# A gated delta layer in a decoder kernel: two column tiles at once in the block solve, output products between its parts, and two elementwise products on GpSimd

## The chip, the cores and the metric

The kernel runs on one core of a Trainium2 chip. The metric is the device time of one execution in microseconds; lower is better. The whole decoder is one program; the change touches one of its twelve sublayers.

## The reference

The program is a four-layer decoder on 2048 tokens of width 256. The sublayer concerned is the attention of layer 1, a gated delta rule with 16 batches of 128 tokens, 16 value heads in 8 key groups, head size 128, all in float32:

```python
def step(S, xs):                      # per batch and value head, token by token
    qt, kt, vt, gt, bt = xs
    S = S * jnp.exp(gt)[..., None, None]
    kv = jnp.einsum('bhk,bhkv->bhv', kt, S)
    delta = (vt - kv) * bt[..., None]
    S = S + jnp.einsum('bhk,bhv->bhkv', kt, delta)
    o = jnp.einsum('bhk,bhkv->bhv', qt * scale, S)
    return (S, o)
...
xf = o.astype(jnp.float32) * jax.nn.silu(z.astype(jnp.float32))
var = jnp.mean(xf * xf, -1, keepdims=True)
xn = xf * jax.lax.rsqrt(var + NORM_EPS) * norm_weight
return xn.reshape(B, T, VALUE_DIM) @ w_out.T
```

Ahead of it stand the projection of q, k, v and z, a causal convolution of four taps with SiLU, and the normalisation of q and k.

## The kernel before

The recurrence is not run token by token. For each batch and head, the 128 tokens form a lower triangular system: a 128x128 matrix of key products, weighted by decays and by beta, is inverted in blocks and applied to the values. A *round* `i` handles one key group for half of the batches: 8 batches times 2 value heads, 16 *slots* of 128x128. There are 16 rounds. In code, `h` is a half of a round (8 slots), `q` a quarter (4 slots, one bank of PSUM).

One round goes as follows. TensorE transposes the values (`turn_values`, L1214), multiplies keys with keys and queries (`multiply_keys`, L1220). VectorE multiplies the products by the decays `e` to get `aT` and `att` (L1653). GpSimd masks `aT` into `al` (L1187). The diagonal 16x16 blocks of `aT` go through memory into `blk` (SyncE's DMAs) so that VectorE can invert all of them at once (`invert`, from L1672), and the results come back through memory as `x0` and `xT0`. Meanwhile TensorE projects the next round's q, k and v (`project`, L1200), turns the previous round's gated outputs (`turn_output`, L1231), projects z (L1208), and multiplies the first half of the outputs by `wo` (`project_out`, L1237). VectorE, behind the inversion, scans the next round's decays (`scan`, L1648) and runs the next round's convolution as steps of one tap (`convolve`, L1593), adds the outputs to `x` (`add`, L1731), and makes `p1` (L1767).

The inverse is then put together from the blocks on TensorE in 64x64 tiles: products `e1`, `xT1`, `wT`, `xT2` (all L1243), each with a copy on ScalarE or VectorE behind it. Between `e1` and `xT1` stand the second half of the output products and the sums of squares of the next round's q and k (`sum_squares`, L1226), which need ScalarE's `squares` (L1448), which needs `silu` of the convolved q and k.

The block solve (`solve`) applies the inverse to the values: `upper` (L1261) for the first 64 rows, `across` (L1265) for their part in the last 64 rows, and `lower` (L1269) for the last 64 rows; ScalarE copies the results to `uw` (L1529, L1532) and VectorE adds (L1778). Then come the outputs (L1388), VectorE's gating with z (`gate`, L1718), and their sums of squares, from which ScalarE makes `rs` (L1470, L1472). `scale_gated` (L1726) multiplies the gated values by `rs`, for `turn_output` in the next round; `weigh` (L1640) multiplies the next round's decays by `beta`, behind ScalarE's exponential (`decay_exp`, L1452), for the next round's `aT`.

The order of work on each engine is written out by hand; engines wait for each other by semaphores, named after what has been done. The layer's work on TensorE, in order:

```python
previous_out(1)                      # L1368
if i:
    next_sums()
pe.wait_ge(s["p1_made"], i + 1)
...
solve(i)                             # L1384
```

Of the kernel before, what the change touches and what calls it, by code (L numbers as in the profile page):

```python
# [996 lines left out]
def layer1_delta(nc, g):  # L997
    with Layer(nc, "l1a") as L:
# [58 lines left out]
        def quarter(n):  # L1057
            return ps[:, 4 + n, :].rearrange("p (k n) -> p k n", n=128)

        in_rounds = gt[1].rearrange("p b h -> p (b h)")  # L1060

# [103 lines left out]
        @block.gpsimd  # L1165
        def _(pool):
            P = nc.gpsimd

            def scale_out(k):
                pool.wait_ge(s["wo_loaded"], 16 * k + 16)  # L1170
                P.tensor_scalar(wo[:], wo[:], nw[:, 0:1], -1.0, ALU.mult, ALU.mult).then_inc(s["wo_scaled"], 1)

            P.memset(raw[:, :, :, 0:CONV - 1], 0.0).then_inc(s["const"], 1)
            P.memset(eps[:], 1e-6).then_inc(s["const"], 1)
            P.memset(y[:], 0.0).then_inc(s["const"], 1)
            pool.wait_ge(s["const"], 3)
            P.memset(y[:, 0:PITCH:BLK + 1], 1.0).then_inc(s["zeroed"], 1)
            P.memset(x0[:], 0.0).then_inc(s["zeroed"], 1)
            P.memset(xT0[:], 0.0).then_inc(s["zeroed"], 1)
            pool.wait_ge(s["rest_loaded"], 16 * 4)  # L1180
            scale_out(0)
            for i in range(ROUNDS):
                for h in range(2):
                    if i:
                        pool.wait_ge(s["r_made"], 4 * i)
                    pool.wait_ge(s["a_made"], 2 * i + h + 1)
                    P.tensor_tensor(heads(al, h), heads(aT, h), bc(outer[:], 1, HALF), ALU.mult).then_inc(s["al_made"], 1)  # L1187
                if i % 2 == 0 and i:
                    scale_out(i // 2)

        @block.tensor
        def _(pe):
# [40 lines left out]

            def project_out(h):
                for b in range(4):
                    for r in range(2):
                        mm = MM(unit(h)[:, b * 256:(b + 1) * 256], oT[:, HALF * h + 2 * b + r, :], wo[:, r, :], start=r == 0, stop=r == 1)  # L1237
                mm.then_inc(s["out"], 1)

# [19 lines left out]
            def upper(q, k):  # L1259
                slot = 4 * q + k  # L1260
                return MM(quarter(q)[0:64, k, :], xT2[0:64, slot, :], vt[0:64, slot, :], start=True, stop=True)  # L1261

# [4 lines left out]
            def lower(q, k):  # L1267
                slot = 4 * q + k
                return MM(quarter(q)[64:128, k, :], xT2[64:128, slot, :], vt[64:128, slot, :], start=True, stop=True)  # L1269

            def solve(i):

                pe.wait_ge(s["xT2_out"], 2 * i + 1)
                for q in range(2):
                    for k in range(4):
                        mm = upper(q, k)
                    mm.then_inc(s["u_made"], 1)
                pe.wait_ge(s["xT2_out"], 2 * i + 2)
                for q in range(2):
                    pe.wait_ge(s["u_out"], 4 * i + q + 1)  # L1280
                    for k in range(3):
                        across(q, k)
                        upper(q + 2, k)
                    across(q, 3).then_inc(s["r_made"], 1)
                    upper(q + 2, 3).then_inc(s["u_made"], 1)
                for q in range(2):
                    pe.wait_ge(s["u_out"], 4 * i + q + 3)
                    pe.wait_ge(s["vr_made"], 4 * i + q + 1)
                    for k in range(3):
                        lower(q, k)  # L1290
                        across(q + 2, k)
                    lower(q, 3).then_inc(s["w_made"], 1)
                    across(q + 2, 3).then_inc(s["r_made"], 1)
                for q in range(2, 4):
                    pe.wait_ge(s["vr_made"], 4 * i + q + 1)
                    for k in range(4):
                        mm = lower(q, k)
                    mm.then_inc(s["w_made"], 1)

            def round_(i):  # L1300
# [39 lines left out]

                def previous_out(h):
                    if not i:
                        return
                    if h == 0:
                        pe.wait_ge(s["wo_scaled"], (i - 1) // 2 + 1)
                    pe.wait_ge(s["oT_out"], 2 * i - 1 + h)
                    project_out(h)

# [17 lines left out]
                for h in range(2):  # L1366
                    slot_half(4, h, diagonal(al), within(x0)).then_inc(s["e1_made"], 1)
                previous_out(1)  # L1368
                if i:
# [12 lines left out]
                if i == 0:  # L1382
                    next_sums()
                solve(i)  # L1384
                for h in range(2):
# [41 lines left out]
        def _(act):  # L1427
# [54 lines left out]
            def round_(i):  # L1482
# [44 lines left out]
                for q in range(4):  # L1527
                    act.wait_ge(s["u_made"], 4 * i + q + 1)
                    A(lows(uw, q), quarter(q)[0:64], ACT.Copy).then_inc(s["u_out"], 1)  # L1529
                for q in range(4):  # L1530
                    act.wait_ge(s["w_made"], 4 * i + q + 1)
                    A(highs(uw, q), quarter(q)[64:128], ACT.Copy).then_inc(s["w_out"], 1)  # L1532
            act.wait_ge(s["ba"], 1)
# [40 lines left out]
        def _(v):  # L1574
# [60 lines left out]

            def weigh(i, h):
                k, b0 = i // 2, batch0(i) + 4 * h
                t = heads(e, h).rearrange("p (b r) n -> p b r n", r=2)
                v.wait_ge(s["decay_exp"], 2 * i + h + 1)
                V.tensor_tensor(t, t, bc(beta[:, b0:b0 + 4, 2 * k:2 * k + 2], 3, 128), ALU.mult).then_inc(s["e_made"], 1)  # L1640

            def scan(i, h):
# [80 lines left out]

            def scale_gated(i, h):
                v.wait_ge(s["g_rs"], i + 1)
                V.tensor_tensor(heads(go, h), heads(go, h), bc(rs[:, HALF * h:HALF * h + HALF], 2, 128), ALU.mult).then_inc(s["normed"], 1)  # L1726

            def add(i, h):
# [7 lines left out]
            def round_(i):  # L1736
# [14 lines left out]
                for h in range(2):  # L1751
                    take_products(i, h, att, 1).then_inc(s["att_made"], 1)
                if i:
                    for h in range(2):
                        scale_gated(i - 1, h)
                invert(i)
# [14 lines left out]
                for h in range(2):  # L1771
                    v.wait_ge(s["xT2_made"], 2 * i + h + 1)
                    V.tensor_tensor(heads(xT2, h), half_out(3, h), heads(xT1, h), ALU.add).then_inc(s["xT2_out"], 1)
                if i:
                    add(i - 1, 1)
                for q in range(4):
                    v.wait_ge(s["r_made"], 4 * i + q + 1)
                    V.tensor_tensor(highs(vt, q), quarter(q)[64:128], highs(vt, q), ALU.add).then_inc(s["vr_made"], 1)  # L1778
                if more:
                    for h in range(2):  # L1780
                        weigh(i + 1, h)

# [8 lines left out]
            for h in range(2):  # L1791
                scan(0, h)
            for h in range(2):
                weigh(0, h)
            for i in range(ROUNDS):
# [2571 lines left out]
```

## Time and profile before

| | |
|---|---|
| median of the runs shown (2412.61 to 2426.64) | 2424.78 us |
| span of the profiled execution, first to last instruction | 2424.5 us |
| TensorE matmul busy | 2112.7 us (87%) |
| VectorE busy | 1856.6 us (77%) |
| ScalarE busy | 1477.2 us (61%) |
| GpSimd busy | 216.2 us (9%) |
| one steady round of the delta layer | 54.79 us |

The profiled execution's own time is its span; nothing else around it is recorded. Busy shares are averages over twelve sublayers with different limits. In the profile, PE is the matmul side of TensorE and PEld its weight load, DVE is VectorE, ACT ScalarE, POOL GpSimd and SPq SyncE's queue of DMA issues. A float32 product appears as two matmul records, and merged rows give the number of records as x16. In timelines the bracket tells the engine's idle time ahead of the row and what ended it.

### The profile page before, as it was taken

The page shows a single profiled execution, that of the slowest core. Times are in us where ns is not written, and L with a number is a line of the kernel's source. Part 1 is how long each engine was busy: PE and PEld are TensorE (multiplying, and loading weights), DVE is VectorE, ACT ScalarE, POOL GpSimd, SP SyncE. Part 2 cuts the span into 40 slices and gives each one's busy share as a digit, 9 for nine tenths or more (in the row PEclk, how much of TensorE's full clock was granted, in tenths as well). Part 3 has the DMA queues.
Part 4 walks back from the last instruction along what each step waited for, and adds up shares of the span by engine and source line. Part 5 has one row for each costly group of instructions (what it writes and reads, how often), then busy time and mean ns, then how long its engine had stood idle before and what let it go on. Part 6 is the DMA issues. An engine that isn't in the chain of part 4 may idle for free. (4 is left out here: it accounts for less than half of the span.)

```text
span 2424.5 us, 42274 instructions
## 1 busy us (share of the span) xinstructions
PE 2112.7 (87%) x16920; PEld 1596.5 (66%) x16920; DVE 1856.6 (77%) x3341; ACT 1477.2 (61%) x2466; POOL 216.2 (9%) x163
## 2 busy tenths in 40 slices
PE   7997447999999999999986589899999996888855
PEld 4666325777777777878774345788888873555633
DVE  4776667888989898889867834478888776678697
ACT  3664255667777777776736631577777775455365
POOL 0000100000100010101100042000000000100313
PEclk8998768999999999999988799999999996999977
DMA  3000012222222221222116355311010000200001
GB/s 159 2 1 12 13 34 53 72 83 57 64 56 66 56 64 54 62 74 80 36 49 212 129 143 176 115 32 57 23 27 6 5 18 1 81 2 1 16 1 35
DMA packets 164785, 135.14 MB, mean 56 GB/s; under 512 B 118512, under 2 KB 145776, under 8 KB 157936
## 3 DMA queue, kind: packets, MB, share of 16 engines
q1 hardware_dynamic: 160752, 126.02, 16.6%
q0 software_dynamic: 3840, 6.43, 1.4%
q8 instruction: 135, 2.21, 0.4%
q14 instruction: 58, 0.48, 0.1%
HBM read 106.42 MB, written 25.98 MB: 55 GB/s over the span
## 5 line engine op out<-in xcount | busy, mean ns | idle before, releaser
L1593 DVE SCALAR_TENSOR_TENSOR ctx_chan<-l1a_raw,l1a_cw,ctx_chan 128x1024 f32<-128x1024 f32 x192 | 232.0, 1279 | 3.5 <-issue 3.5
L1200 PE MATMUL banks<-x_chan,l1a_wp 128*128 128x512 f32 x512 | 225.2, 598 | 4.8 <-ACT l1a_vt L1488 4.8
L1200 PEld LDWEIGHTS banks<-x_chan,l1a_wp 128*128 128x128 f32 x512 | 98.0, 192 | 122.6 <-issue 116.7
L3166 PE MATMUL banks<-x_chan,more_weights_ahead 128*128 128x128 f32 x1024 | 123.6, 275 | 1.2 <-ACT l2a_kT L2693 1.2
L3166 PEld LDWEIGHTS banks<-x_chan,more_weights_ahead 128*128 128x128 f32 x1024 | 121.6, 192 | 3.9 <-ACT l2a_kT L2693 2.0
L1187 POOL TENSOR_TENSOR l1a_al<-l1a_aT,l1a_outer 128x1024 f32<-128x1024 f32 x32 | 75.0, 2364 | 483.2 <-DVE l1a_aT L1653 483.2
L1237 PE MATMUL banks<-l1a_wo,l1a_oT 128*128 128x256 f32 x512 | 117.7, 383 | 0.0
L2706 ACT ACTIVATE l2a_masked<-l2a_masked,l2a_rowmax 128x128 f32<-128x128 f32 x256 | 99.0, 392 | 28.9 <-DVE l2a_rowmax L2919 28.9
L3202 PE MATMUL banks<-l2a_wo,l2a_oT 128*128 128x256 f32 x512 | 114.5, 382 | 0.0
L1208 PE MATMUL banks<-l1a_wz,x_chan 128*128 128x256 f32 x512 | 113.4, 380 | 0.0
L3202 PEld LDWEIGHTS banks<-l2a_wo,l2a_oT 128*128 128x128 f32 x512 | 96.2, 190 | 14.3 <-issue 1.0
L1237 PEld LDWEIGHTS banks<-l1a_wo,l1a_oT 128*128 128x128 f32 x512 | 96.5, 191 | 13.6
L1208 PEld LDWEIGHTS banks<-l1a_wz,x_chan 128*128 128x128 f32 x512 | 96.4, 191 | 12.9 <-issue 0.5
L1436 ACT ACTIVATE l1a_raw<-banks 128x1024 f32<-128x1024 f32 x64 | 65.5, 1024 | 48.8 <-PE banks L1200 48.8
L126 PE MATMUL banks<-ident,x_tok 128*128 128x128 f32 x224 | 43.2, 357 | 40.2 <-ACT x_tok L194 18.4
L3470 ACT ACTIVATE l3a_probsT<-banks 128x512 f32<-128x512 f32 x64 | 38.1, 596 | 59.5 <-PE banks L3636 59.5
L1466 ACT ACTIVATE l1a_oT<-l1a_go 128x1024 f32<-128x1024 f32 x32 | 33.9, 1058 | 64.6 <-DVE l1a_go L1718 64.6
L1778 DVE TENSOR_TENSOR l1a_vt<-banks,l1a_vt 64x512 f32<-64x512 f32 x64 | 44.4, 694 | 37.1 <-PE banks L1265 37.1
L1648 DVE TENSOR_TENSOR_SCAN l1a_e<-ctx_tok 128x1024 f32<-128x1024 f32 x32 | 71.4, 2275 | 1.4 <-DMA ctx_tok<-l1a_rows_mem 1.4
L1438 ACT ACTIVATE ctx_chan<-banks,l1a_cw 128x1024 f32<-128x1024 f32 x64 | 71.0, 1110 | 0.0
L126 PEld LDWEIGHTS banks<-ident,x_tok 128*128 128x128 f32 x224 | 34.3, 185 | 48.7 <-ACT x_tok L194 19.8
L1265 PE MATMUL banks<-l1a_uw,l1a_al 64*64 64x128 f32 x512 | 65.4, 280 | 0.3 <-ACT l1a_uw L1529 0.3
(648 smaller groups left out, 5644.1 us busy)
## 6 DMA issues: line engine op xcount, KB each, us to landing
l1a_sq<-l1a_norm_mem SPq DMA_DIRECT2D x16, 1024.0 KB, 4.7
ctx_tok<-l1a_rows_mem SPq DMA_DIRECT2D x16, 1024.0 KB, 8.1
l1f_wgu<-in_l1f_wgu_dram SPq DMA_DIRECT2D x4, 1408.0 KB, 11.4
moe_sums<-l1x_zero SPq DMA_DIRECT2D x2, 2176.0 KB, 18.3
ctx_chan<-in_ctxT_dram SPq DMA_DIRECT2D x2, 2048.0 KB, 13.8
l1a_wp<-in_l1a_wp_dram SPq DMA_DIRECT2D x8, 512.0 KB, 5.5
l1f_wgu<-moe_sums SPq DMA_DIRECT2D x8, 512.0 KB, 7.5
x_chan<-in_xT_dram SPq DMA_DIRECT2D x4, 512.0 KB, 5.2
```

The source lines that it names most:

```text
L126: mm = nc.tensor.transpose(g.ps[:, n % 2, t * 128:(t + 1) * 128], g.x[:, t0 + t, c * 128:(c + 1) * 128], g.ident[:])
L1187: P.tensor_tensor(heads(al, h), heads(aT, h), bc(outer[:], 1, HALF), ALU.mult).then_inc(s["al_made"], 1)
L1200: mm = MM(projected(i, u)[:, q * 512:(q + 1) * 512], wp[:, c, u * 128:(u + 1) * 128], g.xT[:, c, t0:t0 + 512], start=c == 0, stop=c == 1)
L1208: mm = MM(unit(2 + h)[:, b * 256:(b + 1) * 256], g.xT[:, c, t0:t0 + S], wz[:, c, :], start=c == 0, stop=c == 1)
L1237: mm = MM(unit(h)[:, b * 256:(b + 1) * 256], oT[:, HALF * h + 2 * b + r, :], wo[:, r, :], start=r == 0, stop=r == 1)
L1436: A(raw[:, u, :, CONV - 1:], now, ACT.Copy)
L1438: A(conv[:, u, :], projected(i, u), ACT.Copy, scale=cw[:, c, CONV - 1:]).then_inc(s["tap"], 1)
L1593: V.scalar_tensor_tensor(t, raw[:, u, :, j:j + S], cw[:, c, j:j + 1], t, ALU.mult, ALU.add).then_inc(s["conv_done" if step == 2 else "conv ...
L1648: V.tensor_tensor_scan(heads(e, h).rearrange("p k n -> p (k n)"), rows[:, h * 1024:(h + 1) * 1024], floor, 0.0, ALU.add, ALU.max).then_inc ...
L2706: ins = A(probs[:, k, :], masked[:, k, :], ACT.Exp, bias=rowmax[:, k:k + 1], scale=128 ** -0.5, accum_out=rsum[:, k:k + 1])
L3166: mm = mm_(ps[:, 4 + q % 2, k * 128:(k + 1) * 128], wq[:, c, SHARE * q + k, :], g.xT[:, c, tile(i)], start=c == 0, stop=c == 1)
L3202: mm = mm_(ps[:, 6, 0:D], oT[:, h, :], wo[:, h, :], start=h == 0, stop=h == HEADS - 1)
```

## The change

Four things are changed in the delta layer, and nothing elsewhere.

1. In the solve, `upper` of quarters 0 and 1 alternate, and `lower` of quarters 2 and 3. For that, quarter 1's upper result is written to PSUM partitions 64 to 127 and quarter 3's lower result to partitions 0 to 63, so that the two use different column tiles of TensorE. ScalarE's copies read them there.
2. The second half of the output products is cut in four batches: two stay ahead of the sums of squares, one is issued behind the first upper products, one ahead of the last lower products. Its semaphore is raised at the end of the last one, and VectorE's `add(i - 1, 1)` stands behind the solve's additions instead of ahead of them.
3. `weigh` and `scale_gated` are issued on GpSimd instead of VectorE, behind the two `al` products of the round and ahead of `scale_out`.
4. The last lower products wait for all four of VectorE's additions at once.

```diff
+        def upper_rows(q):
+            return quarter(q)[64:128] if q == 1 else quarter(q)[0:64]
+        def lower_rows(q):
+            return quarter(q)[0:64] if q == 3 else quarter(q)[64:128]
...
+            def weigh(i, h):
+                k, b0 = i // 2, batch0(i) + 4 * h
+                t = heads(e, h).rearrange("p (b r) n -> p b r n", r=2)
+                pool.wait_ge(s["decay_exp"], 2 * i + h + 1)
+                P.tensor_tensor(t, t, bc(beta[:, b0:b0 + 4, 2 * k:2 * k + 2], 3, 128), ALU.mult).then_inc(s["e_made"], 1)
+            def scale_gated(i, h):
+                pool.wait_ge(s["g_rs"], i + 1)
+                P.tensor_tensor(heads(go, h), heads(go, h), bc(rs[:, HALF * h:HALF * h + HALF], 2, 128), ALU.mult).then_inc(s["normed"], 1)
...
+            pool.wait_ge(s["gates_made"], 2)
+            for h in range(2):
+                weigh(0, h)
             for i in range(ROUNDS):
                 for h in range(2):
                     if i:
                         pool.wait_ge(s["r_made"], 4 * i)
                     pool.wait_ge(s["a_made"], 2 * i + h + 1)
                     P.tensor_tensor(heads(al, h), heads(aT, h), bc(outer[:], 1, HALF), ALU.mult).then_inc(s["al_made"], 1)
+                if i:
+                    for h in range(2):
+                        scale_gated(i - 1, h)
+                if i + 1 < ROUNDS:
+                    for h in range(2):
+                        weigh(i + 1, h)
                 if i % 2 == 0 and i:
                     scale_out(i // 2)
...
-                for q in range(2):
-                    for k in range(4):
-                        mm = upper(q, k)
-                    mm.then_inc(s["u_made"], 1)
+                for k in range(3):
+                    upper(0, k)
+                    upper(1, k)
+                upper(0, 3).then_inc(s["u_made"], 1)
+                upper(1, 3).then_inc(s["u_made"], 1)
+                between(2, 3)
                 pe.wait_ge(s["xT2_out"], 2 * i + 2)
...
-                for q in range(2, 4):
-                    pe.wait_ge(s["vr_made"], 4 * i + q + 1)
-                    for k in range(4):
-                        mm = lower(q, k)
-                    mm.then_inc(s["w_made"], 1)
+                between(3, 4)
+                pe.wait_ge(s["vr_made"], 4 * i + 4)
+                for k in range(3):
+                    lower(2, k)
+                    lower(3, k)
+                lower(2, 3).then_inc(s["w_made"], 1)
+                lower(3, 3).then_inc(s["w_made"], 1)
...
-                previous_out(1)
+                previous_out(1, 0, 2)
                 if i:
                     next_sums()
...
-                solve(i)
+                solve(i, lambda first, stop: previous_out(1, first, stop))
...
-                    A(lows(uw, q), quarter(q)[0:64], ACT.Copy).then_inc(s["u_out"], 1)
+                    A(lows(uw, q), upper_rows(q), ACT.Copy).then_inc(s["u_out"], 1)
...
-                    A(highs(uw, q), quarter(q)[64:128], ACT.Copy).then_inc(s["w_out"], 1)
+                    A(highs(uw, q), lower_rows(q), ACT.Copy).then_inc(s["w_out"], 1)
...
-                if i:
-                    for h in range(2):
-                        scale_gated(i - 1, h)
                 invert(i)
...
-                if i:
-                    add(i - 1, 1)
                 for q in range(4):
                     v.wait_ge(s["r_made"], 4 * i + q + 1)
                     V.tensor_tensor(highs(vt, q), quarter(q)[64:128], highs(vt, q), ALU.add).then_inc(s["vr_made"], 1)
-                if more:
-                    for h in range(2):
-                        weigh(i + 1, h)
+                if i:
+                    add(i - 1, 1)
```

## Rows read from the trace of the kernel before

**Rows 1.** One steady round as one window: busy time of each engine, granted clock

```profile
core 0: us, PE busy (x) PEld busy (x) DVE busy (x) ACT busy (x) POOL busy (x), PEclk, DMA share, GB/s
875.87:930.66 54.79, 54.79 (x538) 42.90 (x537) 48.88 (x57) 39.16 (x45) 5.11 (x3) 1.00 0.22 60
```

**Rows 2.** Timeline of that round: start us, duration us, engine, line

```profile
877.62 3.62 PE L1220 MATMUL banks<-ctx_chan 128*128 128x256 f32 x16
...
881.28 1.23 DVE L1653 TENSOR_TENSOR l1a_aT<-banks,l1a_e 128x1024 f32<-128x1024 f32 x1 [0.45 <-PE banks L1220]
...
886.41 0.21 ACT L1472 ACTIVATE l1a_rs<-l1a_rs 128x16 f32<-128x16 f32 x1
...
889.58 0.18 DVE L1672 COPY l1a_y<-l1a_blk 128x8 f32<-128x8 f32 x1 [0.29 <-DMA l1a_blk<-l1a_blk_mem]
...
889.86 0.17 DVE L1677 TENSOR_TENSOR l1a_part<-l1a_blk,l1a_y 128x8 f32<-128x8 f32 x1
...
894.81 1.91 PE L1231 MATMUL banks<-ident,l1a_go 128*128 128x128 f32 x16
...
900.71 9.63 DVE L1593 SCALAR_TENSOR_TENSOR ctx_chan<-l1a_raw,l1a_cw,ctx_chan 128x1024 f32<-128x1024 f32 x8
900.83 1.06 ACT L1452 ACTIVATE l1a_e<-l1a_e 128x1024 f32<-128x1024 f32 x1 [1.02 <-DVE l1a_e L1648]
...
909.02 3.72 PE L1237 MATMUL banks<-l1a_wo,l1a_oT 128*128 128x256 f32 x16
909.90 1.91 ACT L1448 ACTIVATE l1a_sq<-ctx_chan 128x2048 f32<-128x2048 f32 x1
...
911.39 1.22 DVE L1767 TENSOR_TENSOR l1a_p<-l1a_ec,l1a_fold 128x1024 f32<-128x1024 f32 x1
...
912.67 1.07 PE L1226 MATMUL banks<-l1a_sq,ones 128*32 128x512 f32 x8
...
913.67 2.08 PE L1243 MATMUL banks<-l1a_xT,l1a_p 64*64 64x64 f32 x64
...
925.95 2.36 DVE L1640 TENSOR_TENSOR l1a_e<-l1a_e,l1a_beta 128x1024 f32<-128x1024 f32 x2
```

**Rows 3.** Timeline of TensorE in the block solve one round later

```profile
974.22 1.96 PE L1261 MATMUL banks<-l1a_vt,l1a_p 64*64 64x128 f32 x16
...
976.32 0.27 PE L1265 MATMUL banks<-l1a_uw,l1a_al 64*64 64x128 f32 x1
...
976.43 0.27 PE L1265 MATMUL banks<-l1a_uw,l1a_al 64*64 64x128 f32 x1
...
981.78 3.84 PE L1388 MATMUL banks<-l1a_uw,l1a_att 128*128 128x128 f32 x32
```

**Rows 4.** Line L1187, GpSimd's product: ns min/median/max of 32

```profile
L1187 POOL TENSOR_TENSOR l1a_al<-l1a_aT,l1a_outer x32: 2342/2363/2382, 377.1 to 1212.8; 128x1024 f32<-128x1024 f32 x32
```

**Rows 5.** Timeline of layer 3's tail, VectorE and GpSimd

```profile
2284.51 5.85 DVE L4092 SCALAR_TENSOR_TENSOR l3e_o<-l3e_o,l3e_rstd,more_weights_ahead 128x256 f32<-128x256 f32 x4
...
2328.51 1.67 DVE L4092 SCALAR_TENSOR_TENSOR l3e_o<-l3e_o,l3e_rstd,more_weights_ahead 128x256 f32<-128x256 f32 x4
```

**Rows 6.** The same stretch on GpSimd's own timeline

```profile
2284.62 2.59 POOL L3794 TENSOR_TENSOR more_weights_ahead<-more_weights_ahead,l3e_gb 128x1024 f32<-128x1024 f32 x1 [1.81 <-DVE l3e_o L4086]
2287.29 2.40 POOL L3796 TENSOR_TENSOR more_weights_ahead<-more_weights_ahead,l3e_gb 128x1024 f32<-128x1024 f32 x1
```

**Rows 7.** Line L1171 on GpSimd, first and seventh of eight, and VectorE beside it

```profile
336.04 0.70 POOL L1171 TENSOR_SCALAR l1a_wo<-l1a_wo,l1a_nw 128x512 f32<-128x512 f32 x1 [4.26 <-DMA l1a_wo<-in_l1a_wo_dram]
...
1093.21 2.23 POOL L1171 TENSOR_SCALAR l1a_wo<-l1a_wo,l1a_nw 128x512 f32<-128x512 f32 x1 [43.16 <-DMA l1a_wo<-in_l1a_wo_dram]
...
1092.61 2.35 DVE L1633 SCALAR_TENSOR_TENSOR ctx_chan<-ctx_chan,l1a_sq 128x1024 f32<-128x1024 f32 x2
```

**Rows 8.** TensorE after a long wait in the last round: timeline, windows

```profile
1217.73 3.67 PE L1231 MATMUL banks<-ident,l1a_go 128*128 128x128 f32 x16 [6.96 <-DVE l1a_go L1726]
...
1218.00:1220.00 2.00, 2.00 (x11) 0.50 0.27 74
```

More of the change, by code:

```diff
@@ L1232, in turn_output, with project_out @@
                 mm.then_inc(s["o_turned"], 1)
-            def project_out(h):
-                for b in range(4):
+            def project_out(h, first=0, stop=4):
+                for b in range(first, stop):
                     for r in range(2):
                         mm = MM(unit(h)[:, b * 256:(b + 1) * 256], oT[:, HALF * h + 2 * b + r, :], wo[:, r, :], start=r == 0, stop=r == 1)
-                mm.then_inc(s["out"], 1)
+                if stop == 4:
+                    mm.then_inc(s["out"], 1)
             def tile64(bank, lhsT, rhs, k, row):
@@ L1260, in upper @@
                 slot = 4 * q + k
-                return MM(quarter(q)[0:64, k, :], xT2[0:64, slot, :], vt[0:64, slot, :], start=True, stop=True)
+                return MM(upper_rows(q)[:, k, :], xT2[0:64, slot, :], vt[0:64, slot, :], start=True, stop=True)
             def across(q, k):
@@ L1268, in lower, with solve @@
                 slot = 4 * q + k
-                return MM(quarter(q)[64:128, k, :], xT2[64:128, slot, :], vt[64:128, slot, :], start=True, stop=True)
-            def solve(i):
+                return MM(lower_rows(q)[:, k, :], xT2[64:128, slot, :], vt[64:128, slot, :], start=True, stop=True)
+            def solve(i, between):
                 pe.wait_ge(s["xT2_out"], 2 * i + 1)
-                for q in range(2):
-                    for k in range(4):
-                        mm = upper(q, k)
-                    mm.then_inc(s["u_made"], 1)
+                for k in range(3):
[4 more added lines that the diff above has]
+                between(2, 3)
                 pe.wait_ge(s["xT2_out"], 2 * i + 2)
@@ L1339, in round_, with previous_out @@
                     gate_project(i, h)
-                def previous_out(h):
+                def previous_out(h, first=0, stop=4):
                     if not i:
@@ L1346, in previous_out @@
                     pe.wait_ge(s["oT_out"], 2 * i - 1 + h)
-                    project_out(h)
+                    project_out(h, first, stop)
                 def next_sums():
@@ L1634, in normalise @@
                                        ALU.mult).then_inc(s["kq_normed"], 1)
[L1636 to L1640, printed above, removed]
             def scan(i, h):
@@ L1722, in sum_gated @@
                 V.tensor_reduce(ss[:, HALF * h:HALF * h + HALF], heads(oT, h), AX.X, ALU.add).then_inc(s["gsum"], 1)
-            def scale_gated(i, h):
-                v.wait_ge(s["g_rs"], i + 1)
-                V.tensor_tensor(heads(go, h), heads(go, h), bc(rs[:, HALF * h:HALF * h + HALF], 2, 128), ALU.mult).then_inc(s["normed"], 1)
             def add(i, h):
@@ L1792, in _ @@
                 scan(0, h)
-            for h in range(2):
-                weigh(0, h)
             for i in range(ROUNDS):
```

## The prediction

> **What bounds the kernel now.** I read the profile's busy shares first, then one steady round of the delta layer as a single window, then the timeline of that round. In the window TensorE is busy for 54.79 of 54.79 us at the full granted clock, VectorE for 48.88 [rows 1]. So TensorE's instruction stream is the bound, and 16 rounds of it are some 880 us of the 2424.5. But a full TensorE is no proof of slack elsewhere, so the timeline is read for the second-latest path into each TensorE wait. It runs through VectorE. The product of keys ends at 881.24 and VectorE makes the second half of aT from it by 882.51; the diagonal blocks go to memory and back, and the first instruction of the inversion starts at 889.58, having waited 0.29 us for that transfer, not for VectorE. From there VectorE never stops: inversion, two scans, eight convolution steps (900.71 to 910.34), an addition, and p1, which ends at 912.61. TensorE starts the product that needs p1 (xT1) at 913.67, only 1.06 us later. The sums of squares start at 912.67, and their input was ready at 911.81, only 0.86 us earlier [rows 2]. So behind a bound of TensorE stands a second one, of VectorE plus a transfer, about one microsecond away.
>
> **The change part by part.** First, the pairing. Upper products of quarters 0 and 1, and lower products of quarters 2 and 3, run alone today: 16 records in 1.96 us. Two products on different column tiles start every 0.11 us together [rows 3], so 16 records as 8 pairs cost 8 x 0.11 + 0.1 = 0.98. Two places: 2 x 0.98 = 1.96 us less TensorE work per round.
>
> Second, the output products of the second half. They take 912.67 - 909.02 = 3.65 us ahead of the sums; half of them, 1.83, moves into the solve, a batch in each of two places where TensorE would otherwise wait for ScalarE's u copies and VectorE's additions (some 0.8 us each). The solve from its first product to the first of the outputs is 7.56 us (974.22 to 981.78) [rows 3]; after, 7.56 - 1.96 + 1.83, and 0.2 for four more changes between small tiles and the full array (0.1 for the way in and out, from 3.72 against 3.62 us for 16 records of one shape) [rows 2]: 7.63. So the solve is 0.1 longer, and the saving stands ahead of the sums. Bounds: 0.2 shorter if the changes cost nothing, 0.4 longer if an exposed copy is added. The Trainium skill, TensorEngine Tiling (Array Packing), Key Properties, says that changing the tiling mode drains TensorE. That rule speaks against products between tile products; the 0.1 us of the rows is all that the trace shows of it.
>
> Now TensorE comes to the sums at 910.85 instead of 912.67, but the squares end at 911.81 still, since they hang on VectorE's convolution through ScalarE. It starts at 911.87: a gain of 0.8, not 1.83, less the 0.1: 0.7 us a round, if VectorE's path stays as it is.
>
> Third, scale_gated. Off VectorE this saves nothing: its 2.35 us lay in the wait for the blocks' transfer. On GpSimd a product of this shape takes 2.36 us [rows 4] against 1.22. GpSimd is through with al at 885.7, rs comes at 886.62 [rows 2], so the two end at 891.34. TensorE wants them at 894.81 [rows 2]: 3.5 us to spare. The stride of zero in the broadcast is not in rows 4; I take 2.36, with 1.2 (VectorE's) and 3.5 as ends.
>
> Fourth, weigh. VectorE loses 2.36 us at 925.95 [rows 2], and gets add(i-1, 1) behind the solve (1.22). What waits for it next, the product of keys, comes after 16 transposes on TensorE, so this gains nothing on the path. On GpSimd the two products become ready with the decays, at 901.9 and somewhat over a microsecond later than that if the scans are late: in the middle of VectorE's convolution [rows 2]. What queues behind them on GpSimd is scale_out, then al of the next round, all early enough.
>
> **What that does to VectorE.** In layer 3's tail four VectorE instructions with two SBUF inputs and a per-partition scalar take 1.67 us alone, and 5.85 where two GpSimd products of 2.36 us run [rows 5]; the GpSimd ones start 0.11 us after the first of these and take 2.59 and 2.40 [rows 6]. VectorE stood still for 4.18 us, 2.09 for each product, and GpSimd got in between back-to-back instructions. The convolution step has the same form: two SBUF inputs, a scalar from cw. The other way round: a GpSimd scaling takes 0.70 us alone and 2.23 when it arrives while VectorE runs two back-to-back instructions with two SBUF inputs and no scalar; these keep their 2.35 [rows 7]. There GpSimd waited for both. Products with banks as one input ran beside al without a loss (aT, 1.23) [rows 2], so nothing is charged for them. The Trainium skill, SBUF — State Buffer, Who interferes with whom, states the same division: a VectorE instruction with two SBUF inputs contends with a GpSimd one that reads SBUF, one with a single SBUF input doesn't; and by its next rule issue order decides who blocks, which would leave both outcomes below open.
>
> Charged to VectorE's path, per round:
> - Inversion. L1677, with two SBUF inputs, is due at 889.86 and is held until GpSimd's second scaling ends at 891.34, less 0.14 of overlap: +1.3.
> - Convolution. Two GpSimd products get in, 2 x 2.09: +4.2.
> - Squares end at 911.81 + 5.5 = 917.3, sums take 1.07, xT1 starts at 918.4; p1 ends at 912.61 + 5.5 = 918.1 and doesn't decide. Against 913.67: +4.7, and 0.1 for the solve: +4.8.
> - TensorE now waits 917.3 - 910.85 = 6.5 us. After a wait of 6.96 us in the last round the granted clock is 0.50 (1.2 GHz) and 16 transposes take 3.67 us [rows 8] instead of 1.91 [rows 2]: +1.8. Ends: 0, and twice that, 3.6, if it stays low into the solve of small tiles.
>
> Sum: 6.6 us a round, in the 14 rounds (1 to 14) that have all parts: +92.4. Round 0 has the slower weigh in front of its first product (+1.3) and blocked convolutions of which idle time hides about 3 of 4.2; the last round has only the held inversion, 1.3 less what the pairing gives. Together +3. 2424.5 + 95.4 = 2519.9, so 2520. The span of the profiled execution, 2424.5, is within 0.3 us of the median of the runs shown, 2424.78, so the sum needs no correction.
>
> **The rivals.**
> - *GpSimd is kept out of the convolution.* Speaking for it: rows 7; against: the convolution's form is that of rows 5, not of rows 7. Then the first weigh starts beside add(i-1, 0) at about 911.6 and ends at 914.0, p1 is held to 915.0, and xT1 starts at 915.05: +1.4, with the solve +1.5 a round, 14 x 1.5 + 3 = +24: 2448. TensorE's wait is then 3 us, and if the clock falls too, +1.8 a round: 2474.
> - *Only the inversion is held,* because weigh falls in harmless gaps: sums at 913.15, +0.6 with the solve +0.7: 14 x 0.7 + 3 = +13: 2437.
> - *No holding at all: faster.* If the convolution and the small products run at their old speed (steps of 1.28 us) beside GpSimd, the 0.7 us a round stay: 14 x 0.7 = 10, less 1 for round 0: 2416. It decides as soon as the holdings add up to less than 0.7 us a round. At its far end the squares are early as well and all of the 1.96 less the 0.1 counts, 14 x 1.86 = 26: 2398. Rows 5 speak against it.
> - *The pairing doesn't pair.* Both tiles read the same rows of vt's partitions, as the across and upper pair does now, so rows 3 speak against it. It would cost 1.96 us in the solve, 14 x 1.96 = 27 on top of the forecast: 2547.
>
> **How the numbers follow.** GpSimd gets into both places: 0.60, from 2424.5 + 3 + 14 x 4.8 = 2495 to 2424.5 + 3 + 14 x 8.4 = 2545. GpSimd kept out of the convolution: 0.22, half of it below 2449. Inversion only: 0.06. No holding: 0.10, of which 0.04 at its far end. No pairing: 0.02. A measurement of this kernel can tell about 1%, 24 us, from no change. Faster by more: 0.04. Within: 0.06 + 0.06 + 0.11 = 0.23. Slower: 0.73. The range from 2435 to 2545 leaves out no holding below and a tail of about 0.07 above.
>
> **What the profile after would show.** Pairing right: 8 pairs of L1261 in about 1 us. Holding right: VectorE's L1677 of over a microsecond instead of 0.17, or a start that late; two of eight convolution steps of about 3.3 us instead of 1.28; TensorE waiting 5 to 7 us at L1226 for the squares, and a granted clock of 0.5 behind it; rounds of 60 to 62 us. The prediction is wrong if the convolution's durations are unchanged and GpSimd's weigh is long instead (the first rival, p1 late), or if neither is (the third).

## The result, and the profile after

The changed kernel takes 2503.27 us (median of 4, 2502.31 to 2505.78) against 2423.9 us before (median of 4): ratio 1.0345, interval 1.0323 to 1.0367 (the two medians by themselves give 1.0327, inside it). It is some 3.4% slower. Of all executions in this document one, of `weigh_on_vector`, ran in a slow state (3193.06 us at a granted clock of 0.639); the ratios leave it out, and the median of that kernel without it is 2426.80 instead of the 2427.24 given below. The profiled execution has a span of 2504.0 us against 2424.5, so 79.5 us are to be found in the traces. In the delta layer, from the first `al` product of round 1 to that of round 15, the time went from 770.31 to 849.31 us: 79.0 in 14 rounds, 5.6 a round. The rest of the program hardly moved.

The page's first part, engines' busy time over the span:

```profile
span 2504.0 us, 42224 instructions
...
PE 2114.7 (84%) x16869; PEld 1582.5 (63%) x16920; DVE 1845.7 (74%) x3279; ACT 1477.8 (59%) x2466; POOL 353.5 (14%) x225
```

GpSimd is up from 216.2 to 353.5 us and TensorE's busy time is unchanged within 0.1% (2112.7 before). VectorE's is only 10.9 us lower (1856.6 before), although 62 products of 1.2 us went, some 75 us. TensorE and VectorE were given no more work, and the kernel is slower, so the profile has to be read for waits and for instructions that take longer than they should.

One round of 59.81 us as a window, which answers to [rows 1] (columns as there, from one round's first transpose of values to the next's): TensorE, busy for all of 54.79 us before, now idles for 4.9. The mean of the 14 rounds is 60.7 us, against 55.0 before.

```profile
919.58:979.39 59.81, 54.95 (x539) 41.53 (x538) 48.38 (x53) 39.28 (x45) 14.20 (x7) 0.97 0.20 56
```

VectorE's own timeline of this round, which answers to the VectorE rows of [rows 2]:

```profile
933.26 0.93 DVE L1698 COPY l1a_y<-l1a_blk 128x8 f32<-128x8 f32 x1 [2.54 <-DMA l1a_blk<-l1a_blk_mem]
934.10 0.16 DVE L1700 COPY l1a_y<-l1a_blk 128x8 f32<-128x8 f32 x1
...
934.30 0.17 DVE L1703 TENSOR_TENSOR l1a_part<-l1a_blk,l1a_y 128x8 f32<-128x8 f32 x1
...
945.18 12.88 DVE L1625 SCALAR_TENSOR_TENSOR ctx_chan<-l1a_raw,l1a_cw,ctx_chan 128x1024 f32<-128x1024 f32 x8
957.99 1.21 DVE L1753 TENSOR_TENSOR x_tok<-banks,x_tok 128x1024 f32<-128x1024 f32 x1
959.12 1.20 DVE L1786 TENSOR_TENSOR l1a_p<-l1a_ec,l1a_fold 128x1024 f32<-128x1024 f32 x1
```

And GpSimd's two pairs of new products:

```profile
930.40 3.75 POOL L1196 TENSOR_TENSOR l1a_go<-l1a_go,l1a_rs 128x1024 f32<-128x1024 f32 x2 [1.04 <-ACT l1a_rs L1504]
944.25 5.56 POOL L1192 TENSOR_TENSOR l1a_e<-l1a_e,l1a_beta 128x1024 f32<-128x1024 f32 x2 [10.09 <-ACT l1a_e L1484]
```

Read them side by side. The inversion's first copy starts at 933.26, but takes 0.93 us instead of 0.18 [rows 2]: it ends at 934.19, and the first GpSimd pair ends at 934.15. The eight convolution steps take 12.88 us instead of 9.63: +3.25. GpSimd's second pair runs from 944.25 to 949.81, beside the end of the second scan and the first two of them. These two steps alone, from the same timeline in a shorter window:

```profile
945.18 5.71 DVE L1625 SCALAR_TENSOR_TENSOR ctx_chan<-l1a_raw,l1a_cw,ctx_chan 128x1024 f32<-128x1024 f32 x2
```

They take 5.71 us, 2.87 and 2.92 us each where the other steps take 1.27. The second scan and GpSimd's two products one by one:

```profile
943.00 2.27 DVE L1674 TENSOR_TENSOR_SCAN l1a_e<-ctx_tok 128x1024 f32<-128x1024 f32 x1
...
944.25 2.71 POOL L1192 TENSOR_TENSOR l1a_e<-l1a_e,l1a_beta 128x1024 f32<-128x1024 f32 x1 [10.09 <-ACT l1a_e L1484]
...
946.92 2.88 POOL L1192 TENSOR_TENSOR l1a_e<-l1a_e,l1a_beta 128x1024 f32<-128x1024 f32 x1
```

The two engines take turns. The scan keeps its 2.27 us although a product starts inside it; the product ends 1.69 us behind the scan, and the first step stands still meanwhile. The second product ends 1.77 us behind the first step, and holds the second step. So a product waits for the VectorE instruction that is running, and the next VectorE instruction waits for the product. In each of the 14 rounds two of the twelve steps take about 2.9 us, 28 in all; the line's minimum, median and maximum in ns:

```profile
L1625 DVE SCALAR_TENSOR_TENSOR ctx_chan<-l1a_raw,l1a_cw,ctx_chan x168: 1267/1272/2922, 459.0 to 1266.8; 128x1024 f32<-128x1024 f32 x168
```

What follows on ScalarE and TensorE (the squares, then the rest of the outputs, the sums, xT1, wT, and the solve from L1289 to L1420):

```profile
957.62 1.91 ACT L1480 ACTIVATE l1a_sq<-ctx_chan 128x2048 f32<-128x2048 f32 x1
```

```profile
952.73 1.99 PE L1264 MATMUL banks<-l1a_wo,l1a_oT 128*128 128x256 f32 x8
959.58 1.94 PE L1253 MATMUL banks<-l1a_sq,ones 128*32 128x512 f32 x8 [4.86 <-ACT l1a_sq L1480]
961.45 2.57 PE L1271 MATMUL banks<-l1a_xT,l1a_p 64*64 64x64 f32 x64
963.88 2.08 PE L1271 MATMUL banks<-l1a_xT,l1a_ec 64*64 64x64 f32 x64
...
967.69 1.09 PE L1289 MATMUL banks<-l1a_vt,l1a_p 64*64 64x128 f32 x16
968.71 1.13 PE L1264 MATMUL banks<-l1a_wo,l1a_oT 128*128 128x256 f32 x4
...
974.69 1.09 PE L1297 MATMUL banks<-l1a_vt,l1a_p 64*64 64x128 f32 x16
975.71 3.84 PE L1420 MATMUL banks<-l1a_uw,l1a_att 128*128 128x128 f32 x32
```

To compare with [rows 2], lay the two rounds together at the end of the second aT product: 926.21 here, 882.51 before, a shift of 43.70. The squares end at 959.53 - 43.70 = 915.83, before at 911.81: +4.0, which is the 0.73 of the copy and the 3.25 of the convolution. The sums start 3.2 later than before, since they had 0.86 to spare, and TensorE waits 4.86 us for them, where before it hardly waited. The wait in all rounds, total, times, longest:

```profile
PE banks L1253 <- ACT l1a_sq L1480: 68.8, 14, 5.6
```

Behind the wait, the granted clock (third column from the right) in windows of 2 us:

```profile
958.00:960.00 2.00, 0.42 (x4) 0.79 0.00 0
960.00:962.00 2.00, 2.00 (x18) 0.50 0.03 8
962.00:964.00 2.00, 2.00 (x64) 0.86 0.00 0
```

The sums take 1.94 us instead of 1.07, and xT1 starts 1.87 behind them instead of 1.00; its own step to the next line is 2.43 instead of 1.94. That is 1.4 us for the clock. The solve takes 975.71 - 967.69 = 8.02 us instead of 7.56: +0.5. The sum for this round is 3.2 + 1.4 + 0.5 = 5.1. In other rounds the low clock lasts longer, up to all of xT1 (3.68 us busy) and some of what follows. From the start of the sums to the start of the solve the 14 rounds take 8.10 to 9.51 us, 8.9 in the mean, against 6.75 in nearly all rounds before, so over the layer the low clock costs 2.2 us a round and not 1.4. With it the sum is 5.9 above the 54.79 of a steady round; the 14 rounds before took 55.0 in the mean, which leaves the 5.6.

### The profile page after: what moved, and what is told of

Same layout as the page of the kernel before. It is cut to its first block and busy times, and to the rows that moved or that the text cites. A ratio compares the mean times of both kernels' runs of the same rounds, so it can differ in the third digit from the quotient of the medians.

```text
span 2504.0 us, 42224 instructions
## 1 busy us (share of the span) xinstructions
PE 2114.7 (84%) x16869; PEld 1582.5 (63%) x16920; DVE 1845.7 (74%) x3279; ACT 1477.8 (59%) x2466; POOL 353.5 (14%) x225
## 3 DMA queue, kind: packets, MB, share of 16 engines
q8 instruction: 135, 2.21, 0.4%
## 5 line engine op out<-in xcount | busy, mean ns | idle before, releaser
L1625 DVE SCALAR_TENSOR_TENSOR ctx_chan<-l1a_raw,l1a_cw,ctx_chan 128x1024 f32<-128x1024 f32 x192 | 280.7, 1526 | 3.5 <-issue 3.4
L1264 PE MATMUL banks<-l1a_wo,l1a_oT 128*128 128x256 f32 x512 | 126.3, 391 | 0.0
L1192 POOL TENSOR_TENSOR l1a_e<-l1a_e,l1a_beta 128x1024 f32<-128x1024 f32 x32 | 87.6, 2757 | 194.0 <-ACT l1a_e L1484 194.0
L1253 PE MATMUL banks<-l1a_sq,ones 128*32 128x512 f32 x128 | 30.9, 1060 | 79.0 <-ACT l1a_sq L1480 79.0
L1474 ACT ACTIVATE ctx_chan<-ctx_chan 128x1024 f32<-128x1024 f32 x32 | 33.6, 1056 | 70.5 <-DVE ctx_chan L1625 68.6
L1679 DVE TENSOR_TENSOR l1a_aT<-banks,l1a_e 128x1024 f32<-128x1024 f32 x32 | 39.2, 1225 | 43.3 <-PE banks L1247 39.0
```

The source lines that it names most:

```text
L1192: P.tensor_tensor(t, t, bc(beta[:, b0:b0 + 4, 2 * k:2 * k + 2], 3, 128), ALU.mult).then_inc(s["e_made"], 1)
L1625: V.scalar_tensor_tensor(t, raw[:, u, :, j:j + S], cw[:, c, j:j + 1], t, ALU.mult, ALU.add).then_inc(s["conv_done" if step == 2 else "conv ...
```

## The experiments

Two theories stood against that of the held instructions. *Lateness*: GpSimd is slow, and somebody waits for its results. *Solve*: the new order of TensorE's work is longer. In all experiments "on VectorE" puts one half of `weigh` behind the xT2 additions and one behind the solve's additions. Each was timed beside runs of the kernel before on the same chip, which had a median of 2420.2 to 2420.8 us for all ten.

**weigh_on_vector.** `weigh` back on VectorE, `scale_gated` left on GpSimd.

```diff
-                if i + 1 < ROUNDS:
-                    for h in range(2):
-                        weigh(i + 1, h)              # GpSimd
+                if more:
+                    weigh(i + 1, 0)                  # VectorE, ahead of the solve's additions
                 for q in range(4):
                     v.wait_ge(s["r_made"], 4 * i + q + 1)
                     ...
+                if more:
+                    weigh(i + 1, 1)
```

> The changed kernel with weigh back on VectorE (one half behind the xT2 additions, one behind the solve's additions), scale_gated still on GpSimd. Holding theory (GpSimd's reads hold VectorE's instructions with two SBUF inputs): the two convolution steps of 2.92 us go back to 1.27, TensorE's wait for the squares and the low clock behind it go, only the held start of the inversion (0.8 us) stays: 2418 to 2432. Rival, the solve is what got longer (pairing and output products between): stays at 2495 to 2505. Rival, GpSimd is merely late (its products' results are awaited): falls too, so this run does not tell it from holding.

Measured: 2427.24 us, ratio 1.0026 (1.0011 to 1.0042). The solve theory falls: 76 of the 79 us are gone with the solve left as changed. All convolution steps of the 14 rounds are back at their old length (count, busy time, mean ns):

```profile
L1613 DVE SCALAR_TENSOR_TENSOR ctx_chan<-l1a_raw,l1a_cw,ctx_chan 128x1024 f32<-128x1024 f32 x168 | 203.0, 1279 | 0.0
```

**scale_on_vector.** The other way round: `scale_gated` back on VectorE behind the `att` products, `weigh` on GpSimd.

> The changed kernel with scale_gated back on VectorE, weigh still on GpSimd amid the convolution. Holding theory: the inversion's first copy is 0.18 us again, and starts at the transfer: 0.8 us a round less, 14 x 0.8 = 11 below the changed kernel: 2488 to 2496, with the two convolution steps still at 2.9 us. Solve theory: no change, 2500 to 2506.

Measured: 2488.96 us, ratio 1.0288 (1.0255 to 1.0321). The first copy of the inversion is short again in every round (minimum, median, maximum in ns), and the eight convolution steps still take 12.88 us:

```profile
L1691 DVE COPY l1a_y<-l1a_blk x15: 174/175/178, 446.9 to 1282.8; 128x8 f32<-128x8 f32 x15
```

```profile
935.35 12.88 DVE L1618 SCALAR_TENSOR_TENSOR ctx_chan<-l1a_raw,l1a_cw,ctx_chan 128x1024 f32<-128x1024 f32 x8
```

So `scale_gated` on GpSimd costs 14 us beside `weigh`, and 11 us without it (2427.24 against 2416.06 below). Given the intervals of the ratios these two don't differ; 14 rounds of 0.73 us would make 10.

**weigh_late.** All of the change, with one more wait:

```diff
                 if i + 1 < ROUNDS:
+                    pool.wait_ge(s["conv_done"], 4 * (i + 1) + 4)
                     for h in range(2):
                         weigh(i + 1, h)
```

> The changed kernel with one more wait: GpSimd's weigh starts only when all of the next round's convolution is done, in the stretch of the solve where VectorE's inputs come from PSUM on one side. The same GpSimd work, its results some 15 us later. Holding theory: as weigh_on_vector, 2418 to 2432, since only the time of the collision matters. Lateness theory: no better than the changed kernel, 2500 or more.

Measured: 2424.34 us, ratio 1.0019 (1.0007 to 1.0032). GpSimd does the same work and starts `weigh` some 18 us later in the round (37.2 us behind the first `al` product instead of 19.6), and the kernel is 79 us faster than the changed one. The two pairs of GpSimd in one round:

```profile
885.87 3.75 POOL L1196 TENSOR_TENSOR l1a_go<-l1a_go,l1a_rs 128x1024 f32<-128x1024 f32 x2 [1.05 <-ACT l1a_rs L1505]
917.39 3.76 POOL L1192 TENSOR_TENSOR l1a_e<-l1a_e,l1a_beta 128x1024 f32<-128x1024 f32 x2 [27.77 <-DVE ctx_chan L1626]
```

The pair of `weigh` takes 3.76 us here. During the first of the two VectorE runs the xT2 additions, which take one input from PSUM, and they keep their 0.69 us; during most of the second it is idle. Amid scan and convolution the pair took 5.56. So the lateness theory falls, and both engines' instructions were long while they collided.

**both_on_vector.** The pairing and the output products between the solve's parts, with nothing moved to GpSimd.

> Pairing and output products between the solve's parts alone, both elementwise products on VectorE. Holding theory: no held instruction, 0.7 us a round better than before: 2408 to 2418, with TensorE waiting about 1 us a round for the squares. Solve theory: 2495 to 2505. A pairing that costs no wait anywhere would give 2398.

Measured: 2416.06 us, ratio 0.9986 (0.9969 to 1.0004). It lies in the range, but at 0.3 us a round rather than 0.7: the layer's 14 rounds take 766.64 us against 770.31. The interval of the time includes no change; the 0.3 is read from the traces. Timeline of a round, convolution, squares and sums:

```profile
888.80 9.63 DVE L1606 SCALAR_TENSOR_TENSOR ctx_chan<-l1a_raw,l1a_cw,ctx_chan 128x1024 f32<-128x1024 f32 x8
...
898.00 1.91 ACT L1461 ACTIVATE l1a_sq<-ctx_chan 128x2048 f32<-128x2048 f32 x1
...
899.97 1.06 PE L1234 MATMUL banks<-l1a_sq,ones 128*32 128x512 f32 x8 [0.88 <-ACT l1a_sq L1461]
```

The convolution is back at 9.63 us, and TensorE waits 0.88 us for the squares, as worked out. The missing 0.4 is in the solve:

```profile
906.72 1.09 PE L1270 MATMUL banks<-l1a_vt,l1a_p 64*64 64x128 f32 x16
907.74 1.13 PE L1245 MATMUL banks<-l1a_wo,l1a_oT 128*128 128x256 f32 x4
...
914.74 1.49 PE L1401 MATMUL banks<-l1a_uw,l1a_att 128*128 128x128 f32 x11
```

From 906.72 to 914.74 it takes 8.02 us, where the prediction had 7.63. The paired uppers take 1.02 (to 907.74), a saving of 0.84 each and not 0.98, and each batch of output products takes 1.06 with the way in and out, not 0.91 + 0.1.

**spare_products.** To take data and order out of the question, both products stay on VectorE, and GpSimd multiplies a spare tile by itself, twice a round, where `weigh` had been. Nobody reads it.

```diff
+                if i + 1 < ROUNDS:
+                    for h in range(2):
+                        pool.wait_ge(s["decay_exp"], 2 * i + h + 3)
+                        pool.wait_ge(s["spared"], 2 * i + h + 1)
+                        P.tensor_tensor(spare, spare, spare, ALU.mult).then_inc(s["spared"], 1)
```

> Both elementwise products on VectorE, as in both_on_vector, and two further GpSimd products a round of a spare 128x1024 tile with itself, started by the decays as weigh was. Nobody uses the spare tile or waits for these products. Holding theory: two convolution steps of about 2.9 to 3.3 us again, rounds of 59.5 to 61 us, 2480 to 2500. Lateness or solve theory: as both_on_vector, 2408 to 2420.

Measured: 2489.12 us, ratio 1.0289 (1.0266 to 1.0311): the same as scale_on_vector, from work that serves nothing. Mean times over the layer, VectorE's convolution step and GpSimd's product:

```profile
L1614 DVE SCALAR_TENSOR_TENSOR ctx_chan<-l1a_raw,l1a_cw,ctx_chan 128x1024 f32<-128x1024 f32 x167 | 246.9, 1543 | 0.0
```

```profile
L1203 POOL TENSOR_TENSOR ctx_tok<-ctx_tok 128x1024 f32<-128x1024 f32 x28 | 74.3, 2654 | 202.0 <-ACT l1a_e L1473 200.0
```

**spare_memsets.** As above, with four memsets of the spare tile instead, which read nothing.

> As spare_products, but GpSimd writes the spare tile four times a round (4 memsets of 0.95 us) and reads nothing. If what holds VectorE is GpSimd's reading: no held instruction, as both_on_vector, 2408 to 2420. If any GpSimd work on SBUF holds it: 14 x 3.4 = 48 more, 2455 to 2475.

Measured: 2417.78 us, ratio 0.9985 (0.9971 to 1.0000), as both_on_vector. GpSimd writes for 3.8 us a round at the same place, and the convolution step is at its old 1280 ns:

```profile
L1615 DVE SCALAR_TENSOR_TENSOR ctx_chan<-l1a_raw,l1a_cw,ctx_chan 128x1024 f32<-128x1024 f32 x168 | 203.0, 1280 | 0.0
```

```profile
L1204 POOL MEMSET ctx_tok<- 128x1024 f32 x56 | 53.4, 953 | 203.1 <-ACT l1a_e L1474 200.4
```

So what holds VectorE is a GpSimd instruction that reads SBUF; one that only writes it doesn't. The Trainium skill (SBUF — State Buffer, Who interferes with whom) says that an instruction with two SBUF inputs contends with a GpSimd instruction that reads SBUF, "not with one that only writes it"; these two runs agree, with 1543 against 1280 ns.

**spare_in_scan.** As spare_products, started by the end of the inversion instead, so that the first product arrives beside the first of two scans.

> As spare_products, but the two spare products are started by the end of the inversion, so that the first arrives during the first of two scans (VectorE, two SBUF inputs, no per-partition scalar, back to back). If GpSimd gets in between any two VectorE instructions: the second scan takes about 4.2 instead of 2.27 us and one convolution step is long; if it is kept out of a pair without a scalar, as the scaling beside the two normalisations was: both scans 2.27, and the first two convolution steps long. The time is 2480 to 2500 either way.

Measured: 2486.05 us, ratio 1.0268 (1.0247 to 1.0290). The scan's times:

```profile
L1669 DVE TENSOR_TENSOR_SCAN l1a_e<-ctx_tok x28: 2276/3102/3928, 453.0 to 1230.8; 128x1024 f32<-128x1024 f32 x28
```

Every second scan takes up to 3.93 us instead of 2.28, and the first convolution step 2.8 us, so GpSimd gets in between two back-to-back instructions without a scalar too. The scalar isn't what opens the door. Here too the engines take turns: the first scan, during which the product starts, keeps its 2.28 us, and the product is over only 1.7 us behind it. The pair of normalisations that kept GpSimd's scaling out [rows 7] is left unexplained: the instruction kept out there was a scaling with one SBUF input, here it is a product, and no run separates the two.

**pairing_alone.** As both_on_vector, with all output products of the second half ahead of the sums.

> As both_on_vector, but all output products of the second half ahead of the sums, as before the change: the paired products alone. TensorE comes to the sums as late as before; in the solve 1.96 us go and about 0.8 us behind the upper products and 0.9 us ahead of the last lower ones are exposed: 0.15 to 0.3 us a round, 2416 to 2420 where before has 2420. If pairing were worth its TensorE time: 14 x 1.96 = 27 less, 2393.

Measured: 2422.97 us, ratio 1.0009 (0.9997 to 1.0021): no gain, 3 us above the expected range. TensorE's solve:

```profile
916.43 1.09 PE L1270 MATMUL banks<-l1a_vt,l1a_p 64*64 64x128 f32 x16
...
918.29 0.29 PE L1274 MATMUL banks<-l1a_uw,l1a_al 64*64 64x128 f32 x1 [0.77 <-ACT l1a_uw L1542]
...
922.98 1.09 PE L1278 MATMUL banks<-l1a_vt,l1a_p 64*64 64x128 f32 x16 [0.80 <-DVE l1a_vt L1791]
924.00 1.27 PE L1401 MATMUL banks<-l1a_uw,l1a_att 128*128 128x128 f32 x9
```

From 916.43 to 924.00 it takes 7.57 us, before 7.56 [rows 3]. TensorE saves 1.7 us and waits 0.77 for ScalarE's copy behind the uppers and 0.80 for VectorE's last addition ahead of the lowers. The pairing alone turns work into waits; it is the output products between that make something of it.

**moves_alone.** The GpSimd half of the change, with solve and output products as before.

> The other half of the change: weigh and scale_gated on GpSimd as changed, the solve and the output products as before (VectorE's last addition stays behind the solve's). Holding theory: the squares come as late as in the changed kernel, TensorE's shorter solve (7.56 against 8.02 us) gives back 0.46 us a round, and if its wait, now some 3 us, leaves the clock alone another 1.3: 2480 to 2498. If the loss needed the solve's new order too: under 2450.

Measured: 2471.05 us, ratio 1.0205 (1.0179 to 1.0231); a miss by 9 us at the lower end. It is 32 us better than the whole change, although the other half is worth 4 us by itself. The trace tells why:

```profile
941.74 1.07 PE L1253 MATMUL banks<-l1a_sq,ones 128*32 128x512 f32 x8 [3.13 <-ACT l1a_sq L1478]
942.73 2.08 PE L1271 MATMUL banks<-l1a_xT,l1a_p 64*64 64x64 f32 x64
```

With all of its output products ahead of the sums, TensorE waits 3.13 us and not 4.86, and behind that wait the sums take 1.07 us, at the full clock. Nine of the 14 rounds look like this. In five the clock falls all the same, in two of them behind a wait that is no longer:

```profile
588.74 1.93 PE L1253 MATMUL banks<-l1a_sq,ones 128*32 128x512 f32 x8 [3.14 <-ACT l1a_sq L1478]
```

So the length of the wait alone doesn't decide. From the sums to the solve the rounds take 7.3 us in the mean here, 8.9 in the changed kernel, and 6.75 at the full clock. By this the solve's new order costs the changed kernel 0.5 us a round for itself and 1.6 because the clock falls in all rounds behind the longer wait, together some 29 us. My expectation had the clock at 1.3 us a round, from the one round that I had taken apart, where the mean of all rounds is 2.2.

**reordered.** A try at the second bound: `scale_gated` on VectorE, `weigh` on GpSimd as in weigh_late, one pair of convolution steps behind p1, one behind the xT2 additions, the sums behind xT1.

```diff
-                    if more:
-                        convolve(i + 1, 2, 0)
                     add(i - 1, 0)
...
-                    for step in range(1 if i else 0, 3):
+                    for step in range(2 if i else 3):
                         convolve(i + 1, 2, step)
...
+                if i and more:
+                    convolve(i + 1, 2, 2)             # behind the xT2 additions
```

> Pairing and products between, scale_gated on VectorE, GpSimd's weigh behind the whole convolution as in weigh_late; and on VectorE one pair of convolution steps is moved behind p1 and one behind the xT2 additions, the sums of squares behind xT1, with ScalarE's logarithm behind the xT1 copies. If VectorE's chain to p1 is the second bound: xT1 starts up to 2.4 us earlier, of which the sums and the logarithm take back 1.6: 0.6 to 1 us a round better than before, 2406 to 2413. If something else bounds the round: 2414 to 2422.

Measured: 2415.15 us, ratio 0.9976 (0.9962 to 0.9990): faster than before, by 0.2%. That is in the range that I had given for something else bounding the round, 2 us above the one for VectorE's chain. What TensorE waited for over the layer:

```profile
PE banks L1265 <- DVE l1a_p L1786: 6.1, 14, 1.3
PE banks L1265 <- ACT l1a_wT L1546: 2.6, 14, 0.2
```

The waits are short now, 0.4 us for p1 and 0.2 for ScalarE's copies, but the sums now stand between xT1 and the solve, which takes 8.1 us. That these, and the logarithm ahead of ScalarE's wT copies, take the gain is read from the timeline; no run separates them. Of the versions tried this is the only one whose interval lies below 1; it doesn't differ from both_on_vector beyond the uncertainty.

## Why the prediction was right

The forecast was 2520 (2435 to 2545), the measurement 2503. Its likeliest case, that GpSimd gets into both places, is what happened, and the experiments bear out its mechanism. That the sum came within 17 us is in part luck: both holdings were put too high, by 1.5 us a round, and the solve and the clock too low, by 0.8. Point by point:

- *What bounds the kernel.* Right. A second path through VectorE and the transfer lay 0.86 us behind TensorE's, and every delay beyond that came through to the round.
- *Inversion held, +1.3.* Right in kind, 0.73 measured. Two things were off: the scaling takes 1.90 us on GpSimd and not 2.36, so the pair ends at 934.15, 0.9 us behind the transfer and not 1.8; and it is already the copy in front (L1698, one SBUF input) that is held, not the first product with two. The prediction had the section of the Trainium skill (SBUF — State Buffer, Who interferes with whom) say that an instruction with a single SBUF input doesn't contend. The section says so only outside the 2-port perf modes, and names copies among the instructions that can enter these. Whether this copy ran in such a mode no run shows.
- *Convolution held, +4.2.* Right in kind, 3.25 measured: 1.6 for each product instead of 2.09, because these GpSimd products too take 1.9 us alone (3.76 for a pair in weigh_late), not the 2.36 of [rows 4]. The broadcast along the last dimension that I had left open doesn't make GpSimd slower. It isn't what makes it faster either: the spare product has none, and its first one of a round is over 1.7 us behind the scan, as that of `weigh` is. The products of 2.36 us have a second operand that is repeated over heads or groups; no run separates that from the rest.
- *When the products arrive.* Misread: 901.9 is where the second exponential ends. The first is over at 899.82 (898.74 and 1.08 us), so the first product comes during the second scan and not amid the convolution. As it then waits for the scan to end, two steps are held either way.
- *The squares decide, not p1.* Right: TensorE waits at L1253 in all 14 rounds.
- *Clock, +1.8.* Right in kind: 1.4 in the round shown, 2.2 in the mean. TensorE's wait was 4.9 us, a little under the 5 to 7 that were named as a sign. moves_alone, with 0.5 us a round lost to the clock, shows that most of it hung on the output products that had been moved.
- *Solve, +0.1.* Mis-sized: +0.5, from the saving of the pairing (0.84 each, not 0.98) and the batches (1.06 each, not 0.91 and a share of 0.2). By this the whole advantage of the pairing was put at 0.7 us a round, and is 0.3.
- *Sum.* 6.6 us a round forecast, 5.6 measured; 92 against 79 for the 14 rounds. The +3 for rounds 0 and 15 didn't appear: all of the program outside the 14 rounds makes 0.5 us, and round 0 is 1.4 us shorter than before (61.6 us against 63.1 between its first `al` product and the next).
- *Rivals.* "No holding" (2416) is the case of both_on_vector, the change without its GpSimd half. Its 2416.06 meets that number by chance: beside it the kernel before took 2420.22, so the gain is 4 us and not 8. "Only the inversion is held" (2437) is the case of weigh_on_vector, 2427: the held 0.73 costs 11 us and not 21. The pairing does pair. GpSimd is not kept out.

## What to carry to other kernels

Before moving an elementwise product to an idle GpSimd, look at what VectorE runs at that time: beside instructions with two SBUF inputs a GpSimd product that reads SBUF stops VectorE for most of its length, for 1.6 of its 1.9 us. The same product 18 us later in the round, beside instructions that read PSUM or an idle VectorE, held nothing (79 us between these two placings here). And a full TensorE is no proof that taking work off it will pay: measure how far behind it the next path lies (here 0.9 us), and how much of the work taken out was covering a latency (pairing_alone: 1.7 us of work became 1.6 us of waits).

## What the runs showed of the hardware

- A VectorE copy of 128x8 elements with a single SBUF input was held by a GpSimd product as well: 175 ns without it in scale_on_vector, a median of 928 and up to 1044 ns in the changed kernel.
- GpSimd's product of 128x1024 took 2.36 us with a second operand repeated over heads, and 1.90 us with one constant along the last dimension. A plain product of the spare tile with itself held the convolution as long as the latter (2.88 us a step against 2.89).
- After waits of 4.84 us and more TensorE's clock was granted at 0.50 in all 14 rounds of the changed kernel. After waits of 3.12 to 3.22 us in moves_alone the sums ran at the full rate in nine rounds and at the low one in two, and in both_on_vector the clock fell once behind a wait of 2.21 us (0.50 in the window from 736 to 738). Taking 1.7 us of work out from in front of a wait cost 1.6 us a round through the clock.
- In the collision both engines lose, because they take turns, instruction by instruction: `weigh`'s pair took 5.56 us instead of 3.76, VectorE's two steps 5.7 instead of 2.4. The VectorE instruction that is running when the product starts is not lengthened (the scan's 2.27 us).
